# Four of the nine down products of an expert layer computed from split values, three F32R matmuls for one fp32 matmul, with longer lags

## What is computed

```
for e in range(NUM_EXPERTS):                       # 8 routed experts, top 2 of each token
    h = silu(routed @ w1[e].T) * (routed @ w3[e].T)
    out_r += where(m, h @ w2[e].T, 0)
shared = silu(xf @ sw1.T) * (xf @ sw3.T) @ sw2.T   # and one for all tokens
out = shared.at[tok_idx].add(out_r * scores)
```

## Time and profile before

| | us |
|---|---|
| median of 3 runs (lowest, highest) | 794.69 (794.66, 797.31) |
| the profiled execution | 796.4 |
| its span, first to last instruction | 794.3 |
| busy PE, DVE, ACT, POOL | 756.0, 640.6, 520.9, 478.6 |
| mean granted TensorE clock | 0.992 of full |

### The profile page before, as it was taken

The page is one execution under the profiler, slowest core; times in us unless marked ns, Lnnn a source line. Parts: engine busy times, 40 slices in busy tenths (PEclk is TensorE's granted clock), DMA queues, the critical chain, the costliest instruction groups (busy, mean ns, idle before and its releaser), DMA issues. The chain is left out here.

```text
span 794.3 us, 18933 instructions
## 1 busy us (share of the span) xinstructions
PE 756.0 (95%) x6148; PEld 459.3 (58%) x6148; DVE 640.6 (81%) x1386; ACT 520.9 (66%) x1053; POOL 478.6 (60%) x653
## 2 busy tenths in 40 slices
PE   2899999999999999999998989999999999999995
PEld 1345555555555555555554656566666666666663
DVE  7689999999999999999997536867766666666665
ACT  1148889888888888888887636455555545555542
POOL 4345687776766767667533545555655666555554
PEclk9999999999999999999999999999999999999999
DMA  4636776666666566655611734446555555554440
GB/s 116 172 106 169 214 189 180 163 153 173 153 168 170 148 183 155 166 165 143 172 46 38 187 92 112 114 125 121 130 126 128 127 130 124 129 124 130 118 94 26
DMA packets 201446, 108.79 MB, mean 137 GB/s; under 512 B 10392, under 2 KB 200984, under 8 KB 201368
## 3 DMA queue, kind: packets, MB, share of 16 engines
q1 hardware_dynamic: 200048, 105.88, 52.2%
q10 hardware_dynamic: 1320, 1.91, 1.0%
HBM read 73.41 MB, written 33.82 MB: 135 GB/s over the span
## 5 line engine op out<-in xcount | busy, mean ns | idle before, releaser
L1021 DVE TENSOR_REDUCE negmax<-bank 128x2 f32<-128x512 f32 x512 | 320.0, 678 | 14.7 <-PE bank L708 12.2
L560 ACT ACTIVATE probs<-bank 128x512 f32<-128x512 f32 x512 | 292.0, 606 | 60.5 <-PE bank L695 56.6
L671 ACT ACTIVATE q_stack<-k_stack 128x512 f32<-128x512 f32 x128 | 80.7, 631 | 150.8 <-DVE k_stack L1084 149.4
L708 PE MATMUL bank<-k_stack,q_stack 48*128 48x256 bf16 x1024 | 163.3, 282 | 14.0 <-DMA k_stack<-k_parts_dram 9.9
L730 PE MATMUL bank<-x_hi,hi_w 128*128 128x512 f32 x288 | 165.3, 574 | 2.6 <-DVE q_stack L1094 1.8
L695 PE MATMUL bank<-q_stack,k_stack 50*128 50x256 bf16 x1024 | 156.4, 275 | 2.1 <-ACT probs L560 1.5
L1084 DVE TENSOR_TENSOR k_stack<-bank,probs 128x512 f32<-128x512 f32 x128 | 88.2, 689 | 86.2 <-PE bank L732 86.0
L723 PE MATMUL bank<-probs,v_aug 128*32 128x256 f32 x2048 | 138.3, 388 | 0.4 <-ACT attT L571 0.4
L695 PEld LDWEIGHTS bank<-q_stack,k_stack 50*128 50x128 bf16 x1024 | 75.2, 95 | 85.7 <-ACT probs L560 43.9
L731 PE MATMUL bank<-x_hi,lo_w 128*128 128x512 f32 x288 | 114.5, 398 | 0.0
L732 PE MATMUL bank<-x_lo,hi_w 128*128 128x512 f32 x288 | 114.5, 398 | 0.0
(11 more groups left out here) (106 smaller groups left out, 1066.1 us busy)
## 6 DMA issues: line engine op xcount, KB each, us to landing
probs<-route_dram SPq DMA_DIRECT2D x128, 256.0 KB, 4.9
q_stack<-q_parts_dram SPq DMA_DIRECT2D x64, 192.0 KB, 3.3
k_stack<-k_parts_dram SPq DMA_DIRECT2D x64, 192.0 KB, 4.1
k_parts_dram<-k_parts SPq DMA_DIRECT2D x32, 192.0 KB, 2.2
q_parts_dram<-q_parts SPq DMA_DIRECT2D x32, 192.0 KB, 2.1
xT_sb<-xT SPq DMA_DIRECT2D x32, 128.0 KB, 2.2
k_parts_dram<-k_parts SPq DMA_DIRECT2D x32, 128.0 KB, 2.0
q_parts_dram<-q_parts SPq DMA_DIRECT2D x32, 128.0 KB, 2.0
```

The lines of the kernel that those rows point to most:

```text
L560: nc.scalar.activation(probs[h][:], score_ps[EXP_BANK[h]][:].rearrange("p (j t) -> p j t", j=NT), ACT.Exp).then_inc(exp_done, 1)
L671: nc.scalar.activation(act[n % DEPTH], gated[n % DEPTH] if n else up1_ps[0][:], ACT.Silu).then_inc(act_set, 1)
L708: mm = pe.matmul(max_ps[MAX_BANK[h]][:, i * T:(i + 1) * T], q_stack[b.ring][first:last, h // 2, i * P:(i + 1) * P], k_stack[b.ring][first: ...
L1021: nc.vector.tensor_reduce(negmax[b.ring % 2][:, :, column], max_ps[MAX_BANK[h]][:].rearrange("p (i s) -> p i s", i=NT), AX_X, ALU.max, neg ...
```

## The change

Of the nine down products of a group, those of experts 1, 3, 5 and 7 are computed from split values as the up products are: three F32R matmuls in the place of one fp32 matmul. The five others stay as they are. For that

- `w2` of these four is split once, in attention's slot 10 (ACT copies, POOL subtracts).
- per split expert and group ACT makes `hs_hi`, a rounding copy of `hid_s`, two steps behind (`HI_LAG`); the low part `hs_lo` = `hid_s` - `hs_hi` is made by POOL for experts 1 and 5, two steps behind (`POOL_LAG`), and by DVE for 3 and 7, three steps behind (`DVE_LAG`). The two subtractions stand at the end of their step, behind POOL's hid_s and behind DVE's `hidden`.
- `down` is five steps behind `up` and no longer four. `DRAIN_AT`, `TOKENS_AT`, `STATS_AT`, `MEAN_AT` and `NORM_AT` move by one step. `POW_AT` stays 8.
- `hid_s` gets a ring of four, the shared expert's `hid` two buffers of its own, `hs_hi` and `hs_lo` rings of two. POOL's wait before hid_s(n) is for the low part of n-4 where that is split, else for down(n-4).

```
+SPLIT = (1, 3, 5, 7)
+POOL_LO, DVE_LO = (1, 5), (3, 7)
...
-        LAG, HID_LAG = 4, 1
+        LAG, HID_LAG, HI_LAG, DVE_LAG, POOL_LAG = 5, 1, 2, 3, 2
+        HID_RING, SPLIT_RING = 4, 2
...
-        DRAIN_AT, TOKENS_AT, STATS_AT, MEAN_AT, POW_AT, NORM_AT, HI_AT, LO_AT = 3, 5, 6, 7, 8, 1, 3, 4
+        DRAIN_AT, TOKENS_AT, STATS_AT, MEAN_AT, POW_AT, NORM_AT, HI_AT, LO_AT = 4, 6, 7, 8, 8, 2, 3, 4
...
+            def low_part(g, n):
+
+                pool.wait_ge(hs_hi_set, split_done(g, n))
+                k = SPLIT.index(n % NE) % SPLIT_RING
+                pool.tensor_tensor(hs_lo[k][:], hid_s[n % NE % HID_RING], hs_hi[k][:], ALU.subtract).then_inc(hs_lo_pool, 1)
...
-                            pool.wait_ge(down_mm, done(g, n - DEPTH))
+                            used = n - HID_RING if n > HID_RING else n - HID_RING - 1
+                            if used % NE in SPLIT:
+                                wait_lo(pool, g, used)
+                            else:
+                                pool.wait_ge(down_mm, done(g, used))
                         pool.wait_ge(hid_set, done(g, n))
                         pool.wait_ge(square_set, g * E + n)
...
+                    m = behind(g, n, POOL_LAG)
+                    if m is not None and m % NE in POOL_LO:
+                        low_part(g, m)
                     if n == LO_AT and (not isinstance(g, int) or g < GROUPS - 1):
                         split_x(g + 1, 1 - r)
```

The pieces above from `low_part` on are POOL's. ACT's high part, which stands behind `square` and `drain` in its step:

```
+            def high_part(g, n):
+
+                act_e.wait_ge(hids_set, routed(g, n))
...
+                nc.scalar.activation(hs_hi[k % SPLIT_RING][:], hid_s[n % NE % HID_RING], ACT.Copy).then_inc(hs_hi_set, 1)
```

Then `down` on PE:

```
+                if n % NE in SPLIT:
+                    wait_lo(pe, g, n)
+                    k = SPLIT.index(n % NE)
+                    product(down_ps[r], w2_hi[:, k, :], w2_lo[:, k, :], hs_hi[k % SPLIT_RING], hs_lo[k % SPLIT_RING], start=False,
+                            stop=False).then_inc(down_mm, 1)
+                    return
```

And DVE:

```
-            def delayed(g, n):
+            def delayed(g, n, r):
                 m = behind(g, n, HID_LAG)
                 if m is not None:
-                    hidden(g, m)
+                    hidden(g, m, r)
+                m = behind(g, n, DVE_LAG)
+                if m is not None and m % NE in DVE_LO:
+                    low_part(g, m)
```

More of the change, by code:

```diff
@@ L93, in attention_moe_layer @@
         w2_sb = sb("w2_sb", [P, NE, P])
+        w2_hi, w2_lo = (sb(f"w2_{part}", [P, len(SPLIT), P], F32R) for part in ("hi", "lo"))
         ident, ident_bf = sb("ident", [P, P]), sb("ident_bf", [P, P], BF16)
@@ L227, in attention_moe_layer @@
         scores, biased, equal, weights, first_sel = (v.rearrange("p (a e) -> p a e", e=E) for v in take(5))
-        gated, act, hid, hid_s = (take(DEPTH) for _ in range(4))
+        gated, act, hid = (take(DEPTH) for _ in range(3))
+        shared, hid_s = take(2), take(HID_RING)
+        hs_hi, hs_lo = ([sb(f"hs_{part}{r}", [P, G], F32R) for r in range(SPLIT_RING)] for part in ("hi", "lo"))
         weight_b, weight2_b = ([v[:].rearrange("p j t -> p (j t)") for v in probs[n:n + E]] for n in (0, E))
@@ L279, in routed, with split_done, wait_lo, hidden_of @@
             return g * E + (n if n >= 0 else n + 1)
+        def split_done(g, n):
+            n, g = (n, g) if n >= 0 else (n + NE, g - 1)
+            return g * len(SPLIT) + sum(m <= n for m in SPLIT)
+        def wait_lo(engine, g, n):
+            n, g = (n, g) if n >= 0 else (n + NE, g - 1)
+            for by, semaphore in ((DVE_LO, hs_lo_dve), (POOL_LO, hs_lo_pool)):
+                if n in by:
+                    engine.wait_ge(semaphore, g * len(by) + (by.index(n) + 1))
+        def hidden_of(n, r):
+            return hid[n % DEPTH] if n else shared[r]
         def past(g, n):
@@ L675, in group @@
                         drain(g, 1 - r)
+                    m = behind(g, n, HI_LAG)
+                    if m is not None and m % NE in SPLIT:
+                        high_part(g, m)
                     if n == HI_AT and (not isinstance(g, int) or g < GROUPS - 1):
@@ L683, in _ @@
             groups(act_e, group)
+            for n in range(HI_LAG):
+                if (n - HI_LAG) % NE in SPLIT:
+                    high_part(GROUPS, n - HI_LAG)
             drain(GROUPS, 1)
@@ L726, in values, with product @@
                     mm.then_inc(av_mm, 1)
[L728 to L732 removed]
+            def product(ps, of_hi, of_lo, hi, lo, start=True, stop=True):
+                pe.matmul(ps[:], of_hi, hi[:], start=start, stop=False)
+                pe.matmul(ps[:], of_lo, hi[:], start=False, stop=False)
+                return pe.matmul(ps[:], of_hi, lo[:], start=False, stop=stop)
             def up(g, n, r):
@@ L886, in down @@
                 n %= NE
-                pe.matmul(down_ps[r][:], w2_sb[:, n, :], (hid_s if n else hid)[n % DEPTH], start=(n == 0), stop=(n == NE - 1)).then_inc(down_mm, 1)
+                pe.matmul(down_ps[r][:], w2_sb[:, n, :], hid_s[n % HID_RING] if n else shared[r], start=(n == 0), stop=(n == NE - 1)).then_inc(down_mm, 1)
             def by_tokens(g, r):
@@ L1138, in group @@
                         aggregate(g)
-                    delayed(g, n)
+                    delayed(g, n, r)
                     if past(g, 1) and n == STATS_AT:
@@ L1162, in _ @@
             groups(dve, group)
-            for n in range(HID_LAG):
-                delayed(GROUPS, n)
+            for n in range(DVE_LAG):
+                delayed(GROUPS, n, 0)
             norm(GROUPS - 1)
```

44 lines of the change are left out of this document (29 added, 15 removed).

## The result

The changed kernel took 804.01 us (median of 6 runs, 801.47 to 806.16), the kernel before 794.81 in the same session (6 runs, 793.88 to 797.31). The ratio is 1.0109, with a 95% interval of 1.0085 to 1.0132: slower by 9.2 us. The prediction was 799.2 with a range of 789.5 to 806. The result lies in that range, but above the 796 to 802.5 that the prediction gave its own mechanism. The profiled execution took 803.15 us with a span of 801.3.

A forecast was written before the change was run, and what follows sets the result against it. PE's issue was taken to set the pace from group 3 on. Split downs -9.3, down(5) wait +9.1, group 0 +0.2, group 2 0, end +4.5, attention 0: +4.5 on 794.69 gives 799.2 us, range 789.5 to 806.

The forecast's parts named there:

- its own mechanism: The forecast itself, with PE waiting at down(5) in 13 groups: 796 to 802.5 us, chance 0.55.
- The wait at down(5): Steady groups: POOL's low(5) arrives after its deadline, counted from T7 (start of up(7)); 13 x 0.7 = +9.1 us.
- The gain: PE's split downs: three F32R matmuls, 0.70 us, replace a plain down of 0.857; 60 x 0.155 = -9.3 us.
- The lock: DVE and POOL's shared port: low(3) just covered, 0; rival, DVE loses it to hid_s(5): about 815 us, chance 0.12.
- The end: Last group: four downs remain after low(5), +3.6 us, plus half a fall of the clock: +4.5 (3.5 to 5.4).
- Group 0: POOL's low part ahead of the rows PE waits for, offset by waits that go: +0.2 us (0 to 1.3).
- Group 2: Late routing on DVE: hidden(6) earlier, but down(5) about as late as the same point before: 0 (-3.5 to +2).
- The sum: All terms over the whole kernel: +4.5 us, 799.2 us against the median of 794.69.

The follow-up runs named there:

- e1: The changed kernel with POOL making the low part of expert n-2 ahead of hid_s(n) and no longer behind it; 791.0 us.
- e2: The changed kernel with DVE aggregating the statistics behind hidden(7) of step 8 and no longer ahead of it; 792.55 us.
- e8: e1 with all four low parts of a group on POOL and none on DVE; 791.7 us.
- e4: The changed kernel without high or low parts of hid_s: nine plain fp32 downs, only the longer lags and rings left; 794.32 us.
- e3: The changed kernel with all parts made but unused: PE does plain fp32 matmuls of hid_s for all nine downs; 800.47 us.
- e9: The changed kernel with POOL making the normalised rows that PE waits for ahead of hid_s(4) in group 0; 797.96 us.
- e12: e11 with the first block of late routing in group 2 at step 4 and not 3; 788.41 us.
- e7: e10 with group 2's late routing on DVE in four blocks at steps 3, 4, 5 and 6, not two at 3 and 6; 792.5 us.
- e11: The changed kernel with the moves of e1, e2 and e9, a plain down(7) without parts at the end, and late routing in two blocks; 785.91 us.
- e10: The kernel before with POOL making the normalised rows that PE waits for ahead of hid_s(4) in group 0; 790.41 us.

## Why the prediction came out as it did

**The wait at down(5): right, in mechanism and size.** Predicted: operand at T7 + 8.7 against a deadline of T7 + 8.02, 0.7 us in each group. Measured: T7 + 8.67, 0.75 us, and periods of 20.89 against e1's 20.146, 0.74. That holds for ten groups; in groups 3, 1 and 14 it is 0.57, 0.35 and 0.32, and the thirteen make 8.7 us where the sum had 9.1. Of the links, `weigh` came at T7 + 0.95 (predicted 0.89), hidden(7) at 5.24 (5.19), hid_s(7) at 6.09 (6.04), low(5) at 7.33 (7.28): one shift of 0.05 us, at the first, which is the lock (below). e1 and e2 cut the chain at two different places and both end the wait, which shows that it was this chain.

**The gain: right.** 0.153 us for each split product by the periods, 0.155 predicted.

**The lock: right in the steady groups, but for 0.05 us.** Low(3) on DVE was asked for at 612.48 while POOL subtracted for `x_lo` until 613.39, took 1.47 us (681 ns where it was shortest, 1468 in the median of 32) and ended 0.05 us too late: `weigh` of 7 starts at T7 + 0.95 here and at T7 + 0.90 in e8, where T7 is 649.43 and DVE has no subtraction before it:

```profile
650.33 0.69 DVE L1149 TENSOR_TENSOR k_stack<-bank,probs 128x512 f32<-128x512 f32 x1 [1.26 <-PE bank L791]
```

POOL's next multiply took 1.76 instead of 1.28. The period of e8 is that of e1, which has the subtractions. In group 2 the prediction did not look at the lock, and there it was not covered (below). The Trainium skill, page "SBUF — State Buffer", section "Who interferes with whom", says that the order of issue and not the shape decides who blocks. The two rows agree: first DVE was held up by POOL's instruction, which had started, and then POOL by DVE's.

**The end: right in sum, by luck: errors that offset each other.** Timeline of PE there:

```profile
787.83 0.50 PE L788 MATMUL bank<-hs_hi,w_hi 128*128 128x512 f32 x1 [2.84 <-POOL hs_lo L538]
788.16 0.51 PE L789 MATMUL bank<-hs_hi,w_lo 128*128 128x512 f32 x1
788.47 0.63 PE L790 MATMUL bank<-hs_lo,w_hi 128*128 128x512 f32 x1
788.90 1.91 PE L951 MATMUL bank<-v_aug,w_sb 128*128 128x512 f32 x2
789.82 1.42 PE L788 MATMUL bank<-hs_hi,w_hi 128*128 128x512 f32 x1
...
791.46 0.52 PE L790 MATMUL bank<-hs_lo,w_hi 128*128 128x512 f32 x1
791.81 1.02 PE L951 MATMUL bank<-place,w_sb 128*128 128x512 f32 x2
```

The first of these stands at T7 + 8.21 (predicted 8.66), and the last at T7 + 12.19. Between them lie 3.98 us where the prices at the full clock make 2.26, so the lower clock took 1.7 and not the half of it that I had taken (granted 0.83 from 785 to 795). The earlier start, 0.45 us, and a rest that is 0.2 shorter than before offset most of the 0.85.

**Group 0: mis-sized.** The sum had +0.2, with a bound of +1.3. The stretch is 0.75 us longer where four split products should have made it 0.6 shorter, so the term measures 1.4, 1.1 more than the prediction had in this stretch. The rows came 0.35 us later after the first up product, and the wait of PE grew from 2.9 to 4.2 us; then the granted clock was at 0.60 from 460 to 465 and had fallen before 460 already, where before it was 0.66 and 1.00:

```profile
455.00:460.00 5.00, 2.15 (x9) 1.18 (x8) 1.28 (x2) 1.33 (x3) 4.90 (x6) 1.00 0.38 108
```

The place of the rows themselves was nearly right: in e4, with the lags alone, they come 1.1 us earlier than before (17.79 against 18.87 us behind the first up product), and in e3, with the parts, 1.4 later than in e4. From the timeline of PE after that wait:

```profile
458.37 0.66 PE L909 MATMUL bank<-ident,x_new 128*128 128x128 f32 x2 [4.20 <-POOL x_new L507]
...
459.68 0.63 PE L790 MATMUL bank<-x_lo,hi_w 128*128 128x512 f32 x1
460.10 0.63 PE L788 MATMUL bank<-x_hi,hi_w 128*128 128x512 f32 x1
```

Starts 0.42 us apart instead of 0.233: the lower level of 1.2 GHz. Of the 1.4 us the later rows are 0.35, and about 1 is that clock: the term left out what a longer wait would cost in clock. e9 shows what the whole place costs the changed kernel, 6.0 us.

**Group 2: the step that failed.** The prediction looked at the second block of routing and at hidden(6), and took 0. The loss came a block earlier: the stretch from T7 of group 1 to that of group 2 is 2.16 us longer. The waits in the timeline of PE:

```profile
501.31 0.50 PE L788 MATMUL bank<-x_hi,hi_w 128*128 128x512 f32 x1 [0.93 <-DVE q_stack L1159]
503.98 0.50 PE L788 MATMUL bank<-hs_hi,w_hi 128*128 128x512 f32 x1 [1.01 <-POOL hs_lo L538]
```

The first is for hidden(3), the second for low(1). In the steady groups I had checked all nine operands; in group 2 only one. The runs tell the two apart. e4, with longer lags and no parts, has the first wait (0.77 us) and takes 1.03 us more than before from group 1 to group 2 (21.79 against 20.76); so that half comes from the lags. `NORM_AT` moved from 1 to 2, and so the normalisation now stands one step and no longer two ahead of the first block of routing; in e12, with the block one step later, the wait is gone. The normalisation itself also became longer, which the prediction did not have. On DVE before, then after:

```profile
492.22 1.12 DVE L1123 TENSOR_SCALAR place<-place,mv,rstd 128x128 f32<-128x128 f32 x4 [0.38 <-POOL rstd L525]
```

```profile
493.44 2.11 DVE L1194 TENSOR_SCALAR v_aug<-v_aug,mv,rstd 128x128 f32<-128x128 f32 x4
```

It takes 1.1 us in every group before, and 2.1 us in every group from 2 to 15 after; in e4 2.10. In group 2 POOL has a multiply beside it at its new place (from 493.66, 1.29 us) and had none at the old one. The 1.0 us more is the size of e4's loss; that POOL's multiply is the cause is argued, and no run tests it.

The second wait is gone in e1, where low(1) stands ahead of the multiply: it is the order of the two POOL instructions again. But little was won by it, for the first wait is 1.60 us in e1: its transposes of groups 1 and 2 are 1.83 us further apart than its period, those of the changed kernel 2.05. PE meets DVE's delay at one operand or at another. From 490 to 515 us of the changed kernel DVE is busy for 24.1 of 25 us (windows), and part of that is operations that last longer beside POOL: low(3) takes 1.80 us at 503.92 and the first routing operation behind it 1.37, where the same ones take 0.68 and 0.27 alone. e8 has no low part on DVE and still waits 1.61 us at the first place, so that wait isn't the low parts'; at the second it waits 1.54 where e1 waits 2.20. e7, e11 and e12 agree: what is moved within this group comes back as a wait in the next steps.

The miss in this group would have been larger but for the clock. Groups 1 to 3 took 7.0 us more than two periods of e1 in the changed kernel, nearly all of it waits, and 3.8 us more than two periods before, of which 1.7 were the fall of the clock. The changed kernel's execution had no such fall, so its waits grew by 4.9 us where the sum had 0.7 (down(5) of group 1).

**The sum.** In the profiled executions +7.0 against +4.5: group 0 and groups 1 to 3 missed by +1.1, +2.1 and +0.4, the start of the experts came 1.35 us earlier, and all else is within 0.2. That start isn't shown to be the change's: the first up product stands between 438.97 and 446.08 us in the fourteen profiled executions. The other 2.2 us of the medians' difference is how far the two profiled executions are from their medians. That the profiled executions are only 2.5 us off the sum is in part luck: the early start, the fall of the clock that was missing in group 2 and the errors at the end all made the distance smaller.

## What to carry to other kernels

- In an in-order queue, an instruction whose input is ready and whose result is due soon goes ahead of one that waits for a long chain. Here two POOL instructions in the wrong order cost 13 of 804 us, and turned a gain of 0.5% into a loss of 1.1%.
- Write the deadline and the arrival of each new operand down by hand, from rows, in the steady groups and in each special one. The first took the forecast to within 0.03 us; the special group in which it was done for one operand alone was off by 2 us.
- A repair that belongs to the kernel before (e10, 4.6 us from one move) has to be made in both kernels before a change is judged: the split then brings 4.5 us, not 9.

## What the runs showed that I had not expected

The same wait can be followed by the lower clock or not. Before, the wait of 1.80 us at 510.14 was followed by a granted clock of 0.66 in that window. e10 has the same code in group 2 and the same wait (timeline of PE, then the windows):

```profile
505.73 0.50 PE L730 MATMUL bank<-x_hi,hi_w 128*128 128x512 f32 x1 [1.80 <-DVE q_stack L1094]
```

```profile
500.00:505.00 5.00, 3.92 (x14) 2.21 (x12) 4.69 (x19) 0.41 (x1) 2.06 (x2) 1.00 0.55 154
505.00:510.00 5.00, 4.27 (x16) 3.00 (x17) 3.57 (x7) 2.66 (x6) 4.19 (x4) 1.00 0.38 99
```

No fall, and 43.72 us from group 1 to 3 where before took 45.33: 1.6 us, the price of the fall. The changed kernel waited 1.58 us at the same place, and its clock didn't fall either. After 2.20 us in e11 and e1, and 2.5 in e7, it did. What decides at 1.80 is open; a profile of one execution prices such a wait with 1.7 us of clock or without.
